# Local attention with the value product turned round, rows normalised before it, and tile stages over six steps

## The reference

```python
def local_attention(q, k, v):            # 8 heads of 64, windows of 64 tokens
    ...                                  # keys and values: this window and the one before
    sim = jnp.einsum('bhwid,bhwjd->bhwij', bq, bk)
    sim = jnp.where(mask, -jnp.finfo(sim.dtype).max, sim)
    attn = jax.nn.softmax(sim, axis=-1)
    out = jnp.einsum('bhwij,bhwjd->bhwid', attn, bv)

def _layer(x, wqkv, qs, ksc, wo, lg, lb, w1, b1, w2, b2):
    h = shift_token(x)
    q, k, v = jnp.split(h @ wqkv, 3, axis=-1)
    q = l2norm(q) * qs
    k = l2norm(k) * ksc
    q, k = rotary_xpos(q, k)
    o = local_attention(q, k, v)
    x = x + o @ wo
    h = layernorm(shift_token(x)) * lg + lb
    a, g = jnp.split(h @ w1 + b1, 2, axis=-1)
    x = x + (a * jax.nn.gelu(g, approximate=False)) @ w2 + b2
```

## Time and profile before

| | |
|---|---|
| runs | 432.99, 434.39, 436.18 us |
| profiled execution: span, first to last instruction | 431.7 us |
| median of the runs less that span | 2.7 us |
| PE, DVE, ACT, POOL busy | 81%, 74%, 65%, 70% of the span |
| mean granted TensorE clock | 0.941; 1.00 from 98 to 343 us |
| chain that ended last, by engine | PE 37%, DVE 23%, POOL 19%, issue 11%, ACT 7% |

### The profile page before, as it was taken

One profiled execution on the slowest core, in us unless ns is written; L12 is line 12 of the kernel. 1 busy time (PEld: TensorE's weight loads), 2 busy tenths in 40 slices (PEclk: granted clock), 3 DMA queues, 4 the chain that ended last, 5 costly groups with the idle time before them and its releaser, 6 DMA issues.

```text
span 431.7 us, 11030 instructions
## 1 busy us (share of the span) xinstructions
PE 351.5 (81%) x3832; PEld 287.5 (67%) x3832; DVE 321.6 (74%) x751; ACT 280.8 (65%) x844; POOL 301.1 (70%) x247
## 2 busy tenths in 40 slices
PE   1573055899999899999999999999999989988781
PEld 1352034677778687778777887788778867766561
DVE  6889964787689767966796788688869877954653
ACT  3552263688678677867786788678777868764430
POOL 2200419899999889988998699869887988780222
PEclk9996557999999999999999999999999999998966
DMA  7700042412142125112511342043204220220110
GB/s 262 225 0 0 13 125 60 110 27 50 46 118 56 32 55 141 30 30 64 133 32 33 105 94 51 15 121 76 62 3 117 65 53 2 57 57 2 24 49 25
DMA packets 42373, 28.29 MB, mean 66 GB/s; under 512 B 21668, under 2 KB 36566, under 8 KB 42326
## 3 DMA queue, kind: packets, MB, share of 16 engines
q1 hardware_dynamic: 42325, 27.68, 24.4%
HBM read 13.51 MB, written 3.15 MB: 39 GB/s over the span
## 4 chain that ended last, share of the span: by engine, by line
PE 37%; DVE 23%; POOL 19%; issue 11%; ACT 7%; DMA 1%; SPq 1%; POOLq 1%; DVEq 0%; ACTq 0%
POOL rn L507 7%; PE bank L726 5%; POOL rot L552 4%; PE bank L771 4%; DVE rot_sin L1153 4%; PE upper L708 3%; DVE rot_cos L1153 3%; POOL rot L541 3%; ACT probs L902 3%; PE bank L650 2%; PE bank L763 2%; DVE normed L1052 2%; PE upper L659 2%; PE bank L590 2%; DVE neg_max L1201 2%
## 5 line engine op out<-in xcount | busy, mean ns | idle before, releaser
L902 ACT ACTIVATE probs<-upper,neg_max 128x128 f32<-128x128 f32 x256 | 90.4, 369 | 48.5 <-DVE neg_max L1201 48.4
L507 POOL TENSOR_TENSOR rn<-floored,minus_half 128x16 f32<-128x16 f32 x32 | 93.8, 2930 | 2.7
L541 POOL TENSOR_TENSOR rot<-rot_cos,rot_sin 128x512 f32<-128x512 f32 x32 | 40.9, 1277 | 44.3 <-issue 23.6
L1201 DVE TENSOR_REDUCE neg_max<-upper 128x4 f32<-128x512 f32 x64 | 43.1, 684 | 27.5 <-PE upper L708 27.4
L552 POOL TENSOR_TENSOR rot<-rot,rn 128x1024 f32<-128x1024 f32 x32 | 60.9, 1903 | 2.5
L902 ACT ACTIVATION_READ_ACCUMULATOR probs<-upper,neg_max 128x1 f32 x256 | 53.0, 207 | 0.0
L590 PE MATMUL bank<-wqkv_hi,act_t_hi 128*128 128x512 f32 x96 | 43.3, 452 | 7.9 <-DVE act_t_lo L1140 2.8
L1153 DVE TENSOR_TENSOR rot_cos<-bank,tab 128x512 f32<-128x512 f32 x64 | 43.6, 681 | 2.0 <-PE bank L594 1.9
L1153 DVE TENSOR_TENSOR rot_sin<-bank,tab 128x512 f32<-128x512 f32 x64 | 43.4, 679 | 0.0
L542 POOL TENSOR_TENSOR rot<-rot_cos,rot_sin 128x512 f32<-128x512 f32 x32 | 40.9, 1279 | 0.0
L1160 DVE TENSOR_REDUCE ss<-sq 128x16 f32<-128x1024 f32 x32 | 38.7, 1209 | 2.4 <-ACT sq L944 2.3
(11 more groups left out here) (140 smaller groups left out, 863.7 us busy)
## 6 DMA issues: line engine op xcount, KB each, us to landing
v_mid<-v_tok SPq DMA_DIRECT2D x64, 128.0 KB, 2.3
tab_raw<-tables SPq DMA_DIRECT2D x8, 512.0 KB, 3.4
h_tok<-group_in SPq DMA_DIRECT2D x14, 128.0 KB, 3.5
x_res<-group_in SPq DMA_DIRECT2D x28, 64.0 KB, 1.8
wqkv_raw<-wqkv SPq DMA_DIRECT2D x2, 768.0 KB, 6.8
x_in<-x SPq DMA_DIRECT2D x4, 256.0 KB, 3.6
head_scale<-head_scales SPq DMA_DIRECT2D x8, 128.0 KB, 4.0
group_in<-normed SPq DMA_DIRECT2D x4, 256.0 KB
```

The costliest lines, as they stand in the source:

```text
L507: pool.tensor_tensor(rn[:, 0:2 * HEADS], floored[:, 0:2 * HEADS], minus_half[:, :], ALU.pow).then_inc(rn_ready, 1)
L541: pool.tensor_tensor(rot[cur.par][:, :, 0:32], rot_cos[:, :, 0:32], rot_sin[:, :, 32:64], ALU.add).then_inc(rot_added, 1)
L902: last = act.activation(probs[:, h, :], s_bank[half][:, (h % 4) * P:(h % 4 + 1) * P], ACT.Exp, bias=neg_max[a.par][:, h:h + 1], accum_out= ...
L1201: dve.tensor_reduce(neg_max[a.par][:, 4 * half:4 * half + 4], src, AX.X, ALU.max, negate=True).then_inc(max_ready, 1)
```

## The change

- **Value product.** `mix_values` takes v as the stationary operand and the transposed probabilities as the moving one, and so writes o transposed into bank 2. The four transposes of o on PE (`transpose_o`) and the division of o on DVE (`divide_o`) are gone; ACT's `save_o` copies from bank 2 straight into `o_t`.
- **Rows first.** DVE's `normalise_probs` inverts the row sums and multiplies the 128 x 1024 probabilities in SBUF by them, in place, before PE transposes them.
- **Six steps.** Scores stand two steps behind the projection, exponentials and normalisation three, transposes of probabilities and value product four, output projection five. `rot_cos`, `rot_sin`, `ss`, `probs` have two buffers, v five slots. The transposed probabilities go to banks 3 and 4, which also hold the transposes of q and k; PE waits for them to be saved between the two.
- **Order inside a step.** Row maxima both stand first on DVE, and half of the probabilities are saved between the rotations of q and of k. ACT saves v and half of the probabilities between the two halves of the exponentials, and squares q and k after saving q, k and, in j = 3, the next inputs. The next group's inputs move from j = 0 to j = 3.
- **Passes** are written out, without the loop. The ending interleaves the feed-forward part of group 6 with the last tiles, in banks of its own.
- The feed-forward part keeps its step, j = 2, and POOL its order within a step; the `deviation_roots` of a group now come after the tile with number 4G+5 instead of 4G+4, since each step's `cur` is one tile further on.

```diff
+            def normalise_probs(a):
+                dve.wait_ge(exp_done, 2 * a.t + 2)
+                link(dve.reciprocal(inv_sum[:, :], row_sum[a.par][:, :]))
+                dve.tensor_tensor(probs[a.par][:, :, :], probs[a.par][:, :, :],
+                                  inv_sum[:, :].unsqueeze(2).broadcast_to([P, HEADS, P]), ALU.mult).then_inc(probs_ready, 1)
...
-                for h in range(HEADS):
...
-                    for low, v in ((0, v_mid[a.slot]), (64, v_tok[a.slot])):
-                        last = pe.matmul(o_bank[low:low + 64, cols], probs_t[:, h, low:low + 64], v[:, cols],
-                                         start=True, stop=True)
+                for c in range(PAIRS):
+                    for low, v in ((0, v_mid[a.v]), (64, v_tok[a.v])):
+                        for odd in range(2):
+                            head = 2 * c + odd
+                            last = pe.matmul(o_bank[64 * odd:64 * odd + 64, c * P + low:c * P + low + 64],
+                                             v[:, head * DH:(head + 1) * DH], probs_t[:, PAIRS * odd + c, low:low + 64],
+                                             start=True, stop=True)
...
-                    cur, prev, mid, done, after = (At(G, j, back, layer) for back in range(5))
+                    cur, prev, mid, done, after = (At(G, j, back) for back in (0, 2, 3, 4, 5))
...
+                    if cur.valid:
+                        rotate(cur, 0)
+                    if done.valid:
+                        save_probs(done)
+                    if cur.valid:
+                        rotate(cur, 1)
...
+                    if mid.valid:
+                        normalise_probs(mid)
+                    if j == 3 and G + 2 < LAST:
+                        split_inputs(G + 2)
                     if cur.valid:
                         sum_squares(cur)
...
+                    if done.valid:
+                        if j == 3 and G >= 1:
+                            pe.wait_ge(y_read, G)
+                        transpose_probs(done)
                     if after.valid:
                         project_out(after)
...
-            def transpose_o(a, to=None):
```

More of the change, by code:

```diff
@@ L259, in tile @@
-        def tile(t):
[L260 to L279, removed]
-            body(LAST - 1, DEPTH - 1, 2)
+            if value > 0:
+                eng.wait_ge(s, value)
@@ L281, in passes @@
+        def passes(body, ending):
+            for G in range(-1, LAST - 1):
+                body(G)
+            body(LAST - 1, 2)
             ending()
@@ L299, in link @@
                 self.catch_up()
-            def enter(self):
-                self.start, self.n = self.base + self.n, 0
-            def at(self, i, each):
-                self.base, self.each = self.start + i * each, each
-            def leave(self, times):
-                assert self.n == self.each, f"a pass of the loop has {self.n} steps"
-                self.base, self.n = self.start + times * self.each, 0
         def low_pieces(l):
@@ L689, in project_out, with transpose_qk @@
                 last.then_inc(wo_done, 1)
+            def transpose_qk(a, after=None):
+                pe.wait_ge(rot_scaled, a.t + 1)
+                for half, (b, ready, saved) in enumerate(((qt_bank, qt_done, pt_saved0), (kt_bank, kt_done, pt_saved1))):
+                    if after:
+                        pe.wait_ge(saved, after.t + 1)
+                    for p in range(PAIRS):
+                        h = half * HEADS + 2 * p
+                        last = pe.transpose(b[:, p * P:(p + 1) * P], rot[a.par][:, h:h + 2, :].rearrange("p h d -> p (h d)"), ident)
+                    last.then_inc(ready, 1)
@@ new lines, in up @@
+            def up(F, c, banks):
+                c0, cn = CHUNKS[c]
+                layer = F // GROUPS
+                cols = [slice(part * HID + c0, part * HID + c0 + cn) for part in range(2)]
+                for part, (b, w) in enumerate(zip(banks, cols)):
+                    if c == 0:
+                        pe.wait_ge(h2t_saved, 2 * F + 1 + part)
+                    pe.matmul(b[0:cn, :], w1_hi[layer][:, w], h2_hi[:, :], start=True, stop=False)
+                    pe.matmul(b[0:cn, :], w1_lo[layer][:, w], h2_hi[:, :], start=False, stop=False)
+                if c == 0:
+                    pe.wait_ge(h2_split, F + 1)
+                for b, w in zip(banks, cols):
+                    last = pe.matmul(b[0:cn, :], w1_hi[layer][:, w], h2_lo[:, :], start=False, stop=True)
+                last.then_inc(up_done, 1)
```

643 lines of the change are left out of this document (285 added, 358 removed).

## The result

The changed kernel takes 479.5 us (median of four runs, 478.4 to 480.7), the kernel before, run beside it, 433.7 (432.2 to 436.2). The ratio is 1.105, 95% interval 1.100 to 1.110. Forecast were 458 us, in a range from 441 to 468: the direction was right, but the loss is 46 us and not 24.

What follows compares the result with a forecast made beforehand. The prediction took a loop through POOL, not PE, to bound the kernel. Its terms 8.4 + 5.7 - 4.4 + 6.9 + 11.5 - 4.4 = +23.7 us on a span of 431.7, plus 2.7 around it, gave 458 us, range 441 to 468.

Steps and rivals of the forecast that it cites:

- The loop, and that it stays: Each group's period of 42.0 us is a loop through three POOL tiles, roots and PE's feed-forward part; the change keeps its members.
- rival D: PE is the bound after all: POOL's tiles run under the feed-forward part, period 38.7, some 415 us; chance 0.08.
- Start of POOL in j = 3: POOL starts 5.2 us after PE instead of 3.86, behind DVE's copy of transposed probabilities: +1.4 us at each of six marks.
- Sum of squares: In j = 3 ACT's squares and DVE's sum come late, so POOL waits 1.1 us; 5.7 over five periods.
- Waits that go: In j = 0 and 1 POOL finds its tile ready, saving 0.75 us a period; with the hardware loop's turns, -4.4 in all.
- One more tile: In the lead-in the first group's roots come after ten POOL tiles instead of nine: +6.9 us.
- The normalisation: DVE's product with two SBUF inputs holds POOL 0.9 us, 17 times on the loop; three quarters taken: +11.5.
- The split of the feed-forward input: On DVE, now behind the normalisation; starts as before if issued before POOL's add: 0 taken, other end 6.9.
- The ending: From the last mark, one POOL tile is left instead of two: -4.4, bounds -8 and 0.
- B: Rival: locks are short, DVE's normalisations fall into POOL's powers and cost +0 instead of +11.5: 446.6 us; chance 0.22.
- E: Rival: it comes out even; rotation of j = 3 and sum not late, locks free: 432 us; chance 0.08.
- C: Rival: every normalisation is paid (+15.3), and the feed-forward split too (+6.9): 468.8 us; chance 0.10.

Runs made afterwards that it cites:

- the first run: The changed kernel without the product of the probabilities with the inverted row sums, its waits and the reciprocal kept: 458.6 us, ratio 1.056.

## Why the prediction was wrong in size

**The loop, and that it stays.** Right. In the changed kernel POOL is 40% of the chain, and rival D (PE as the bound, 415 us) fell: PE is busy 40.5 of 47.7.

**Start of POOL in j = 3, +1.4.** The size held: 273.62 - 268.37 = 5.25 against 5.2 predicted and 3.86 before. The reason was half right: with DVE's order put back, PE's transposes end the wait at the same time, at 5.19.

**Sum of squares, +1.1 in each of five periods.** Right. POOL takes it 4.33 us after its first add where the earlier trace rows have 3.19: +1.14. The sign named for it, a wait of about 1 us, is not to be seen in the changed kernel, where a hold of 0.99 fills it; with a sum or nothing in the product's place the wait is 1.10. Wait and hold in one place were counted once, as they should be.

**Waits that go, -4.4.** Held in its main part: the 0.75 us a period of the earlier trace rows are gone.

**One more tile, +6.9.** Near. The first roots are at 159.40, 17.9 later than the 141.53 of the kernel before. From POOL's first add to them the run without the product takes 90.04 us, 3.82 of it the wait for tables; without that wait it is 86.2 against 78.7 in the kernel before, so the tile is 7.5. The changed kernel takes 95.69, so its holds there are 5.7. With 3.7 for the tables and 0.9 for the later first add (63.71 for 62.81) that is the 17.9.

**The normalisation, +11.5.** The mechanism was right and is shown; its size by the holds was somewhat too small. Two in a period cost, as counted, and that of j = 3 is hidden, as said; the price of one was good (0.9 predicted, 0.99 measured for an add, 0.77 for a scaling). They make 1.76 us in a period where 1.35 were counted, and 5.7 in the lead-in for 4.7: 14.5 in all. The quarter taken off for powers isn't given, because the product starts when ACT's exponentials end (its reciprocal waits 0.17 for them before 282.41), and that is late in a power, in a scaling or an add: the three starts of a period, 273.82, 282.65 and 290.36, repeat to 0.1 us from one period to the next. The 20.8 us of the run without the product hold 6.0 more by way of PE's clock, which the prediction didn't connect with it. A scaling of 1.90 that begins 0.32 us behind a product of 1.23 takes 2.67. Here the trace agrees with the Trainium skill (SBUF — State Buffer, "Who interferes with whom"), by which one of the two that contend blocks until the other is done. It does not agree for a power that has begun: the product inside it takes its plain 1.23 (last section).

**The split of the feed-forward input, 0.** Held: it is done at 261.02 (259.50 + 1.52), and PE's first product on it starts at 262.06.

**PE's wait before the transposes.** This is the step that failed. The prediction said that "PE should be idle before the transposes of the feed-forward rows, for several us in each group", but has no term for it in the sum: the 12.19 us from the last scaling to the first q product went in unchanged, and with them a TensorE clock that stays up. PE is idle 4.69 us; then its clock is at 0.57 for the next 7.9 us, and PE's feed-forward part is on the loop. From the start of DVE's normalised rows, 255.64, to the first q product, 268.37, are 12.73 us where the kernel before has 10.57 (269.50 to 280.07): +2.2 in each period and in the lead-in, 12.6 us for six (76.0 in all for 63.4). PE kept at work gives 10.2 back.

**Tables.** Not in the prediction: +3.7 at the start. A tile that comes later in SP's order (the loads of the second tables, issued behind all stores of the mixed rows) was not followed through the queue.

**The ending, -4.4.** -1.5 was measured; within its bounds of -8 and 0.

With the measured terms the sum comes near: 23.7 predicted, +12.6 for the clock, +3.0 for the holds (14.5 instead of 11.5), +3.7 for the tables, +0.9 for the first add, +0.6 for the tile and +2.9 for the ending make 47.4, against 46.3 of span. So the clock is more than half of what the forecast missed.

Of the rivals, B (446.6) fell with the first run, E (432) too, and C (468.8), every normalisation paid, came nearest: its 15.3 for them is close to the 14.5 measured, its 6.9 for the split did not come. The warning in the text, "I am wrong if POOL waits longer than 4.2 us for q and k", is what happened: 6.78.

## What to carry to other kernels

When stages are spread over more steps, go through every in-order queue again and ask what is still awaited soon: a consumer that has moved two steps away frees its producer, and whatever stood behind that producer (here roots of 4 columns and a copy of 128 keys) should go first. Free such steps together, since each hides the next: here -9 us for the first alone, -34 for both. And try the move in the other kernel before calling it a general gain: the roots alone are -9 us in one and +10 in the other. Where a wait of PE is gathered in one place, price the clock after it, and not only the wait.

## What the runs showed of the hardware beyond what I expected

- Filling a PE wait with useless products made the kernel 10.2 us faster. After 4.69 us without work the next 7.9 us had a granted clock of 0.57, at which 32 score products took 1.92 us for 1.04; behind a wait of 3.22 us they took 1.92 as well.
- A power of 2.93 us on POOL is held when DVE's product began shortly before it (3.73 us), but one that has begun lets the product pass, and neither is longer for it. It depends on which of the two is first: in the kept traces of all these kernels the 11 powers that began behind a product and beside it take 3.7 to 4.0 us, and all 59 products that began inside a power, 0.7 us or more behind its start, take their plain time, as do those powers. A power and a product inside it, from the kernel with roots and keys early:

```profile
279.55 2.93 POOL L457 TENSOR_TENSOR rn<-floored,minus_half 128x16 f32<-128x16 f32 x1
```

```profile
281.11 1.23 DVE L1148 TENSOR_TENSOR shared<-shared,inv_sum 128x1024 f32<-128x1024 f32 x1
```

- A DVE sum over 1024 columns in SBUF holds nothing of POOL (1.30 for its add), a product over as many, with a second input in SBUF, holds it for about 1.0 us; left alone both take DVE 1.22.
